# A four-block conditioned sequence model on one core: full values kept in PSUM, normalisation and residual sums on GpSimd, loops written out

## The chip, the cores and the metric

One core of one Trainium2 chip runs the kernel. The metric is the device time of the program in microseconds (us); each figure is the median of several runs. All data is float32.

## What is computed

The input x has 16 batches of 256 rows of 256 values. Four conditioned blocks L0 to L3 act on it one after the other. Each is a sum of a residual and gated sub-layers of the same form:

```python
h = layernorm(x) * (1.0 + scale) + shift      # scale, shift, gate from the batch's condition
x = x + gate * (gelu(h @ W1 + b1) @ W2 + b2)   # the feed-forward form
```

L1 puts an attention of 16 heads of 64 ahead of its feed-forward part, L3 an attention of one head of 256. In L2 the first sub-layer's sum replaces x only where a mask (one bit per batch and row) says so. L3's last sub-layer has a second gelu after W2.

## The kernel before

x stays in SBUF for the whole program (128 partitions, 16 batches of 512 columns). The work is eight stages, p in the code:

- stages 0, 1, 3, 4, 5 and 7 are feed-forward (hidden widths 256, 512, 1024, 512, 512, 1024). A group is two batches; a stage has 8 groups. A chunk is 128 hidden units, so a group has 2, 4 or 8 chunks.
- stage 2 is the attention of 16 heads (one pass over the 16 heads per batch), stage 6 the attention of one head.

Products are made exact enough by splitting: every operand is a high part (rounded to fp32r) and a low part, the full value less the high part. `split3` (L255) issues three matmuls for each product. So each activation is evaluated twice on ScalarE, once as the full value and once rounded, and VectorE subtracts.

**One chunk** passes through `ff_hidden` (L547: six 512-wide matmuls into a U bank of PSUM; two U banks), `ff_activate` (L559: full value into hf, rounded value into hh, both from the U bank), `ff_rest` (L570: hl = hf - hh on VectorE) and `ff_output` (L575: twelve 256-wide matmuls into the Y banks; two pairs of banks, used in turn by the groups). Hidden products run two chunks ahead of output products (LOOK = 2).

**One batch's layer norm** passes through `ln_stats` (L306: statistics on VectorE, then the epsilon addition, L326), `ln_rsqrt` (L328: power -0.5 on GpSimd), `ln_norm` (L332: xn = (x - mean) * rstd on VectorE, two instructions), `ln_transpose` (L365: four transposes by TensorE into a T bank), `ln_modulate` (L379: ScalarE, full value into nf and rounded value) and `ln_rest` (L393: the low part on VectorE). Stage 0 and the start of stage 1 have one T bank, the others two; a transpose waits until ScalarE has read the bank (ln_nf).

**One group's residual**: `ff_take` (L596) multiplies the Y bank by the gate into upd on VectorE; GpSimd has made xb = x + gate * bias (L798) meanwhile; `ff_add` (L607) adds them on VectorE. In stage 4 it copies x into act2, copies the mask column into mcur, adds, lets `copy_predicated` overwrite act2 where the mask is set, and copies act2 back to x. In stage 7 ScalarE applies the second gelu (`ff_gelu2`), GpSimd the gate (`ff_gate2`, L644) and VectorE adds (L614).

**The order of the work** is written out by hand: `ff_body` (L693) lists for each engine what it issues in each chunk c of group g. VectorE begins a group with `ff_take` of the group before, does the statistics in chunk 0 or 1, `ln_norm` and the rounding of the next stage's weights (`weights_hi`, L283) in the chunk after, and `ff_add` in chunks 1 to 3. GpSimd does the powers, the weights' low parts (`weights_lo`, L292) and xb. SP issues the loads of gates and weights and the stores. In stage 2, `mh_vector` (L1192) puts `ln_norm` for the next batch into slot 8 of 16 and `mh_gpsimd` (L1226) the power into slot 5; in stage 6, `sh_turn` (L1386) puts `ln_norm` between the low part of v and the score maximum. The inner groups or batches of stages 1 to 7 are hardware loops (`Fori`) with waits against register values; the first and last ones, and all of stage 0, are straight code. Small `memset` instructions on a spacer tile stand between some of VectorE's dependent instructions. Between stages that aren't both feed-forward all engines meet (`end_phase`).

## Time and profile before

| | |
|---|---|
| median of 3 runs | 1963.29 us (1960.59 to 1963.70) |
| profiled execution, span | 1962.5 us |
| TensorE matmuls busy | 1801.1 us (92%) |
| VectorE busy | 1591.7 us (81%) |
| ScalarE busy | 1304.6 us (66%) |
| GpSimd busy | 869.5 us (44%) |
| DMA queues | 12% of 16 engines' span |
| chain that ended last | PE 57%, DVE 20%, issue 12%, ACT 8% |

The span is the time from the first to the last instruction of one profiled execution; the program's own time isn't listed apart for it, and the median of the runs lies 0.8 us above the span. In the rows PE is TensorE, DVE VectorE, ACT ScalarE, POOL GpSimd; L573 is line 573 of the kernel. Names of tiles stand without their buffer numbers, so "bank" is any of the eight banks of PSUM.

### The profile page before, as it was taken

What the parts mean: (1) busy time and instruction counts of PE and PEld (TensorE: products, weight loads), DVE (VectorE), ACT (ScalarE), POOL (GpSimd) and SP (SyncE); (2) the same over time, 40 slices, a digit from 0 to 9 for tenths busy, and PEclk for the clock granted to TensorE, in tenths of its full rate; (3) what the DMA queues carried; (4) which work ended last, traced back from release to release, by engine and by line L of the source; (5) the groups of instructions that cost most, each with busy time, mean ns of one, the idle gap of its engine ahead of it and who ended that gap; (6) DMA issues with size and microseconds to landing.
All of it is one profiled execution on the core that took longest, in us unless ns stands there. A gap on an engine that the chain in (4) does not pass through costs nothing.

```text
span 1962.5 us, 42453 instructions
## 1 busy us (share of the span) xinstructions
PE 1801.1 (92%) x12739; PEld 1656.6 (84%) x12739; DVE 1591.7 (81%) x4130; ACT 1304.6 (66%) x3178; POOL 869.5 (44%) x1009
## 2 busy tenths in 40 slices
PE   6888979999999999999999989999988989989998
PEld 3657879898999999899999988999877879978997
DVE  5888878999999999999999985555899878995563
ACT  3545557777777787777777775555655646656664
POOL 1445545565555555555555543322333533231111
PEclk7999989999999999999999999999999999999999
DMA  8222200000000000000000001110111111211111
GB/s 278 62 62 79 66 18 8 5 8 8 8 8 5 8 3 8 8 8 8 5 8 3 8 7 31 30 37 25 33 42 36 52 44 33 48 41 44 44 43 43
DMA packets 110877, 64.63 MB, mean 33 GB/s; under 512 B 81530, under 2 KB 92788, under 8 KB 110788
## 3 DMA queue, kind: packets, MB, share of 16 engines
q1 hardware_dynamic: 110788, 63.54, 11.9%
q8 instruction: 45, 0.74, 0.2%
q14 instruction: 44, 0.36, 0.1%
HBM read 59.06 MB, written 4.46 MB: 32 GB/s over the span
## 4 chain that ended last, share of the span: by engine, by line
PE 57%; DVE 20%; issue 12%; ACT 8%; DVEq 1%; POOL 1%; DMA 0%; ACTq 0%; POOLq 0%; SPq 0%
PE bank L257 18%; PE bank L258 17%; PE bank L259 17%; DVE smax L1000 4%; PE bank L1042 3%; ACT prob L1014 2%; DVE xn L338 2%; DVE ptlo L1055 2%; PE bank L375 1%; ACT nf L388 1%; PE bank L434 1%; DVE nTlo L395 1%; DVE hl L573 1%; DVE stats L316 1%; DVE x L637 1%
## 5 line engine op out<-in xcount | busy, mean ns | idle before, releaser
L567 ACT ACTIVATE hf<-bank,vecs 128x512 f32<-128x512 f32 x240 | 167.9, 700 | 311.7 <-PE bank L259 305.7
L573 DVE TENSOR_TENSOR hl<-hf,hh 128x512 fp32r<-128x512 f32 x240 | 199.5, 835 | 157.1 <-ACT hh L567 155.4
L1014 ACT ACTIVATE prob<-bank,nmax 128x256 f32<-128x256 f32 x544 | 253.8, 474 | 92.3 <-DVE nmax L1005 92.2
L330 POOL TENSOR_TENSOR rstd<-vareps,mhalf 128x2 f32<-128x2 f32 x128 | 107.0, 836 | 352.4 <-DVE vareps L326 352.2
L967 POOL TENSOR_TENSOR kklo<-qkf,kkhi 128x256 fp32r<-128x256 f32 x128 | 94.2, 736 | 311.1 <-DVE kkhi L953 311.1
L258 PE MATMUL bank<-WBlo,hh 128*128 128x256 f32 x768 | 218.0, 284 | 0.0
L259 PE MATMUL bank<-WBhi,hh 128*128 128x256 f32 x768 | 217.7, 284 | 0.0
L257 PE MATMUL bank<-WBhi,hl 128*128 128x256 f32 x768 | 217.3, 283 | 0.0
L967 POOL TENSOR_TENSOR qzlo<-qkf,qzhi 64x256 fp32r<-64x256 f32 x256 | 208.3, 814 | 10.0
L257 PE MATMUL bank<-pthi,vlo 128*64 128x256 f32 x512 | 159.7, 312 | 48.1 <-ACT of L1074 30.0
L1031 ACT ACTIVATE prob<-prob,rinv 128x256 f32<-128x256 f32 x272 | 138.7, 510 | 94.7 <-DVE rinv L1024 92.7
L1000 DVE TENSOR_REDUCE smax<-bank 128x2 f32<-128x512 f32 x272 | 186.0, 684 | 11.2 <-PE bank L259 9.6
L1051 ACT ACTIVATE pthi<-bank 128x512 fp32r<-128x512 f32 x272 | 161.1, 592 | 42.3 <-PE bank L1042 42.1
L1055 DVE TENSOR_TENSOR ptlo<-bank,pthi 128x512 fp32r<-128x512 f32 x272 | 185.5, 682 | 1.0 <-ACT pthi L1051 0.8
L257 PE MATMUL bank<-nThi,WBlo 128*128 128x512 f32 x384 | 159.1, 414 | 29.1 <-DVE nTlo L395 17.8
L388 ACT ACTIVATE nf<-bank,mod 128x256 f32<-128x256 f32 x256 | 147.6, 577 | 50.2 <-PE bank L375 35.6
L257 PE MATMUL bank<-aThi,WAlo 128*128 128x256 f32 x576 | 164.9, 286 | 11.6 <-DVEq L247 9.1
L567 ACT ACTIVATE hh<-bank,vecs 128x512 fp32r<-128x512 f32 x240 | 167.2, 697 | 0.0
L1042 PE MATMUL bank<-ident,prob 128*128 128x128 f32 x1088 | 164.7, 274 | 2.3 <-DVE prob L1026 2.3
L259 PE MATMUL bank<-aThi,WAhi 128*128 128x256 f32 x576 | 163.9, 285 | 0.0
L258 PE MATMUL bank<-aTlo,WAhi 128*128 128x256 f32 x576 | 163.8, 284 | 0.0
L258 PE MATMUL bank<-nTlo,WBhi 128*128 128x512 f32 x384 | 154.7, 403 | 0.0
(169 smaller groups left out, 6270.8 us busy)
## 6 DMA issues: line engine op xcount, KB each, us to landing
gates<-gate_scratch SPq DMA_DIRECT2D x96, 256.0 KB, 3.5
agate<-gate_scratch SPq DMA_DIRECT2D x32, 256.0 KB, 3.1
stage<-in_L_cond_W SPq DMA_DIRECT2D x64, 64.0 KB, 2.2
out<-x SPq DMA_DIRECT2D x16, 256.0 KB, 2.2
adaw<-in_L_cond_Wc SPq DMA_DIRECT2D x1, 3072.0 KB, 17.7
stage<-in_L_cond_W_qkv SPq DMA_DIRECT2D x8, 384.0 KB, 3.4
x<-in_x SPq DMA_DIRECT2D x1, 2560.0 KB, 16.9
stage<-in_L_cond_ff_w SPq DMA_DIRECT2D x32, 64.0 KB, 2.1
```

Source lines behind the costliest of these rows:

```text
L257: pe.matmul(dst, lhs[1], rhs[0], start=start, stop=False, skip_group_check=True)
L258: pe.matmul(dst, lhs[0], rhs[1], start=False, stop=False, skip_group_check=True)
L259: return pe.matmul(dst, lhs[0], rhs[0], start=False, stop=stop, skip_group_check=True)
L388: last = act.activation(dst, T[:, c * SEQ:(c + 1) * SEQ], ACT.Identity, scale=mod[:, p, 0, c, bass.ds(b, 1)], bias=mod[:, p, 1, c, bass.ds ...
L567: last = act.activation(dst[:, :], U_BANKS[c % 2][:, :], ACTF[p], bias=vecs[:, at:at + 1])
L573: dve.tensor_tensor(hl[r][:, :], hf[r][:, :], hh[r][:, :].bitcast(F32), ALU.subtract).then_inc(h_lo, 1)
L967: return pool.tensor_tensor(dst, src, hi.bitcast(F32), ALU.subtract)
L1000: dve.tensor_reduce(smax[i][:, :], src.rearrange("p (q k) -> p q k", q=TPB), AX_X, ALU.max).then_inc(max_ready, 1)
L1014: last = act.activation(dst[:, q, :], src[:, q * SEQ:(q + 1) * SEQ], ACT.Exp, scale=scale, bias=nmax[i][:, q:q + 1], accum_out=rsum[i][:, ...
L1042: last = pe.transpose(PTB[i][:, c * SEQ + q * P:c * SEQ + (q + 1) * P], src[:, q, c * P:(c + 1) * P], ident[:, :])
L1051: act.activation(pt[i][0][:, :], PTB[i][:, :], ACT.Copy).then_inc(pt_hi, 1)
L1055: dve.tensor_tensor(pt[i][1][:, :], PTB[i][:, :], pt[i][0][:, :].bitcast(F32), ALU.subtract).then_inc(pt_lo, 1)
```

## The change

- **Full values in place.** nf and hf are gone. ScalarE writes the rounded value first and then the full value back over the bank it reads; VectorE subtracts from there. The T bank and the U bank are now held until VectorE's subtraction is done. There are four U banks (0 to 3) in a ring and one pair of Y banks (4 and 5): the first output of a group waits, bank by bank, for `ff_take` of the group before.
- **Normalisation on GpSimd.** The epsilon addition and `ln_norm` move there. The power and the epsilon addition are done for both batches of a group at once, behind the statistics of both.
- **Residual sums on GpSimd.** `ff_add` runs at the head of GpSimd's list in the next group (in stage 7 behind `ff_gate2`), ahead of the norms, the weights and xb. At the end of a stage that isn't followed by a feed-forward one, and at the end of stage 7, it is the last item.
- **Masked rows.** In stage 4 GpSimd writes the sum into act2 and VectorE's `ff_where` copies the masked rows from there straight into x, in chunks 2 and 3; the copies of x and of the mask are gone.
- **Loops written out.** The `Fori` loops are Python loops, and the spacer memsets are gone.

```diff
-        meanvar = [sb(f"meanvar{j}", [P, TPB, 2]) for j in range(GB)]
-        vareps = [sb(f"vareps{j}", [P, TPB]) for j in range(GB)]
-        rstd = [sb(f"rstd{j}", [P, TPB]) for j in range(GB)]
-        mhalf = sb("mhalf", [P, TPB])
+        meanvar = sb("meanvar", [P, GB, TPB, 2])
+        vareps = sb("vareps", [P, GB, TPB])
+        rstd = sb("rstd", [P, GB, TPB])
+        mhalf = sb("mhalf", [P, GB, TPB])
...
-        nf = [sb(f"nf{j}", [P, ROWW]) for j in range(GB)]
...
-        hf = [sb(f"hf{i}", [P, GW], scope=ffn) for i in range(HRING)]
...
-            if p and early(b, 2 * GB + 2):
+            if p:
...
-            dve.wait_ge(ln_mv, u + 1)
-            dve.tensor_scalar(vareps[j][:, :], meanvar[j][:, :, 1], EPS[p], None, ALU.add).then_inc(ln_ve, 1)
-        def ln_rsqrt(pool, p, b, j):
-            pool.wait_ge(ln_ve, p * BATCH + b + 1)
-            pool.tensor_tensor(rstd[j][:, :], vareps[j][:, :], mhalf[:, :], ALU.pow).then_inc(ln_rstd, 1)
-        def ln_norm(dve, p, b, j):
+        def ln_rsqrt(pool, p, b, j, n=1):
             u = p * BATCH + b
-            dve.wait_ge(ln_rstd, u + 1)
+            pool.wait_ge(ln_mv, u + n)
+            pool.tensor_scalar(vareps[:, j:j + n, :], meanvar[:, j:j + n, :, 1], EPS[p], None, ALU.add).then_inc(ln_ve, n)
+            pool.wait_ge(ln_ve, u + n)
+            pool.tensor_tensor(rstd[:, j:j + n, :], vareps[:, j:j + n, :], mhalf[:, j:j + n, :], ALU.pow).then_inc(ln_rstd, n)
+        def ln_norm(pool, p, b, j):
+            u = p * BATCH + b
+            pool.wait_ge(ln_rstd, u + 1)
             if not early(u, sets(p, b)):
-                dve.wait_ge(ln_tp, u + 1 - sets(p, b))
+                pool.wait_ge(ln_tp, u + 1 - sets(p, b))
             for k in range(TPB):
-                last = dve.tensor_scalar(xn[j][:, k * D:(k + 1) * D], x[:, bass.ds(b * ROWW + k * D, D)],
-                                         meanvar[j][:, k, 0:1], rstd[j][:, k:k + 1], ALU.subtract, ALU.mult)
+                last = pool.tensor_scalar(xn[j][:, k * D:(k + 1) * D], x[:, bass.ds(b * ROWW + k * D, D)],
+                                         meanvar[:, j, k, 0:1], rstd[:, j, k:k + 1], ALU.subtract, ALU.mult)
             last.then_inc(ln_xn, 1)
...
+        def pool_norms(pool, units):
+            if units:
+                ln_rsqrt(pool, *units[0], len(units))
+            for n in units:
+                ln_norm(pool, *n)
...
-                pe.wait_ge(ln_nf, u if p == 0 or p == 1 and early(b, 2 * GB + 1) else u + 1 - sets(p, b))
+                pe.wait_ge(ln_lo, u if p == 0 or p == 1 and early(b, 2 * GB + 1) else u + 1 - sets(p, b))
...
-                for dst in (nf[j][:, c * SEQ:(c + 1) * SEQ], hi[c]):
+                for dst in (hi[c], T[:, c * SEQ:(c + 1) * SEQ]):
...
-            dve.tensor_tensor(lo, nf[j][:, :].rearrange("p (c r) -> p c r", c=DC), hi.bitcast(F32),
+            dve.tensor_tensor(lo, t_bank(p, b, j)[:, :].rearrange("p (c r) -> p c r", c=DC), hi.bitcast(F32),
...
-        U_BANKS, Y_BANKS = bank[0:2], [bank[2:4], bank[4:6]]
+        U_BANKS, Y_BANKS = bank[0:HRING], bank[4:6]
...
-            if not early(n, 2):
-                pe.wait_ge(h_act, n - 1)
+            if not early(n, HRING):
+                pe.wait_ge(h_lo, n + 1 - HRING)
...
-            for dst in (hf[r], hh[r]):
-                last = act.activation(dst[:, :], U_BANKS[c % 2][:, :], ACTF[p], bias=vecs[:, at:at + 1])
+            for dst in (hh[r], U_BANKS[r]):
+                last = act.activation(dst[:, :], U_BANKS[r][:, :], ACTF[p], bias=vecs[:, at:at + 1])
...
-            dve.tensor_tensor(hl[r][:, :], hf[r][:, :], hh[r][:, :].bitcast(F32), ALU.subtract).then_inc(h_lo, 1)
+            dve.tensor_tensor(hl[r][:, :], U_BANKS[r][:, :], hh[r][:, :].bitcast(F32), ALU.subtract).then_inc(h_lo, 1)
...
-            if c == 0 and not early(GROUP_BASE[p] + g, 2):
-                pe.wait_ge(y_taken, GB * (GROUP_BASE[p] + g - 1))
             for r in range(GB * TPB):
-                last = split3(pe, Y_BANKS[i][r // TPB][:, (r % TPB) * D:(r % TPB + 1) * D],
+                if c == 0 and r % TPB == 0 and not early(GROUP_BASE[p] + g, 1):
+                    pe.wait_ge(y_taken, GB * (GROUP_BASE[p] + g - 1) + r // TPB + 1)
+                last = split3(pe, Y_BANKS[r // TPB][:, (r % TPB) * D:(r % TPB + 1) * D],
...
+        def ff_add(pool, p, g):
+            for j in range(GB):
                 n = GB * (GROUP_BASE[p] + g) + j
                 b = GB * g + j
                 if p == L3_FF:
-                    dve.wait_ge(gated2, n - GB * GROUP_BASE[L3_FF] + 1)
-                    dve.tensor_tensor(xs(b), xs(b), act2[:, j, :], ALU.add).then_inc(x_new, 1)
+                    pool.wait_ge(gated2, n - GB * GROUP_BASE[L3_FF] + 1)
+                    pool.tensor_tensor(xs(b), xs(b), act2[:, j, :], ALU.add).then_inc(x_new, 1)
                     continue
-                dve.wait_ge(y_taken, n + 1)
-                dve.wait_ge(xb_ready, n + 1)
+                pool.wait_ge(y_taken, n + 1)
+                pool.wait_ge(xb_ready, n + 1)
                 if p == L2_SSM:
-                    dve.memset(spacer[:, 2 + j:3 + j], 0.0)
-                    dve.tensor_copy(act2[:, j, :], xs(b))
-                    dve.tensor_copy(mcur[:, j, :], maski[:, bass.ds(b * TPB, TPB)])
-                    dve.tensor_tensor(upd[:, j, :], upd[:, j, :], xb[:, j, :], ALU.add).then_inc(x_tmp, 1)
-                    dve.wait_ge(x_tmp, 2 * b + 1)
-                    dve.memset(spacer[:, 4 + j:5 + j], 0.0)
-                    for k in range(TPB):
-                        last = dve.copy_predicated(act2[:, j, k * D:(k + 1) * D],
-                                                   mcur[:, j, k:k + 1].to_broadcast([P, D]),
-                                                   upd[:, j, k * D:(k + 1) * D])
-                    last.then_inc(x_tmp, 1)
-                    dve.wait_ge(x_tmp, 2 * b + 2)
-                    dve.memset(spacer[:, 6 + j:7 + j], 0.0)
-                    dve.tensor_copy(xs(b), act2[:, j, :]).then_inc(x_new, 1)
+                    pool.tensor_tensor(act2[:, j, :], upd[:, j, :], xb[:, j, :], ALU.add).then_inc(x_tmp, 1)
                 else:
-                    dve.tensor_tensor(xs(b), upd[:, j, :], xb[:, j, :], ALU.add).then_inc(x_new, 1)
+                    pool.tensor_tensor(xs(b), upd[:, j, :], xb[:, j, :], ALU.add).then_inc(x_new, 1)
+        def ff_where(dve, p, g, batches=range(GB)):
+            for j in batches:
+                b = GB * g + j
+                dve.wait_ge(x_tmp, b + 1)
+                for k in range(TPB):
+                    last = dve.copy_predicated(x[:, b * ROWW + k * D:b * ROWW + (k + 1) * D],
+                                               maski[:, b * TPB + k:b * TPB + k + 1].to_broadcast([P, D]),
+                                               act2[:, j, k * D:(k + 1) * D])
+                last.then_inc(x_new, 1)
...
-                            for n in norms:
-                                ln_norm(eng, *n)
...
-                        if C == GB and c == 1 and prev:
-                            ff_add(eng, *prev)
-                        if C > GB and 2 <= c < 4 and prev:
-                            ff_add(eng, *prev, [c - 2])
+                        if 2 <= c < 4 and prev and prev[0] == L2_SSM:
+                            ff_where(eng, *prev[:2], [c - 2])
...
-                    for n in norms:
-                        ln_rsqrt(eng, *n)
+                    if prev and p == L3_FF:
+                        ff_gate2(eng, p, g - 1, 1 - i)
+                    if prev:
+                        ff_add(eng, *prev[:2])
+                    pool_norms(eng, norms)
...
-            with eng.Fori(1, GROUPS // 2 - 1) as pair:
-                for i in range(2):
-                    body(eng, p, 2 * pair + i, i, 2)
+            for g in range(2, GROUPS - 2):
+                body(eng, p, g, g % 2, GROUPS - 1 - g)
...
-                if i == 8 and not last:
-                    ln_norm(dve, A, b + 1, 0)
...
+                    ln_norm(pool, A, b + 1, 0)
...
-            with eng.Fori(1, BATCH - 1) as b:
+            for b in range(1, BATCH - 1):
...
-                    ln_norm(eng, *sh_batch(b + 3), n)
...
+                    ln_norm(eng, *sh_batch(b + 3), n)
...
-            with eng.Fori(1, BATCH // 2 - 2) as pair:
-                for i in range(2):
-                    sh_turn(name, eng, 2 * pair + i, i, 3)
+            for b in range(2, BATCH - 4):
+                sh_turn(name, eng, b, b % 2, BATCH - 1 - b)
```

## Rows read from the trace of the kernel before

**Rows 1.** Table of stretches: start:end, length, busy (instructions) per engine, clock, DMA, GB/s.
```profile
20.00:144.70 124.70, 100.85 (x485) 69.60 (x486) 93.31 (x302) 63.85 (x121) 47.23 (x50) 0.86 0.37 110
144.70:253.25 108.55, 93.46 (x589) 84.23 (x587) 93.36 (x188) 59.55 (x110) 62.14 (x45) 0.95 0.26 73
298.27:1093.98 795.71, 753.98 (x5998) 723.55 (x5997) 723.24 (x1822) 623.18 (x1794) 455.69 (x561) 1.00 0.03 7
1211.91:1375.43 163.52, 163.52 (x1063) 149.17 (x1062) 96.65 (x246) 95.39 (x168) 48.05 (x56) 1.00 0.12 32
1375.43:1500.88 125.45, 109.09 (x662) 98.34 (x661) 112.77 (x351) 73.09 (x135) 45.47 (x46) 0.93 0.13 38
1500.88:1602.64 101.76, 93.58 (x600) 84.34 (x599) 89.82 (x241) 61.82 (x115) 51.70 (x56) 0.98 0.18 49
1635.87:1734.93 99.06, 94.02 (x750) 89.52 (x749) 93.55 (x266) 66.14 (x166) 31.83 (x44) 1.00 0.21 44
1765.00:1962.50 197.50, 189.29 (x1208) 171.88 (x1208) 108.05 (x226) 115.58 (x201) 33.14 (x31) 0.98 0.14 43
55.81:144.69 88.88, 73.66 (x382) 52.52 (x382) 73.53 (x228) 43.13 (x82) 39.18 (x40) 0.92 0.24 62
1529.18:1541.54 12.36, 12.36 (x82) 11.17 (x81) 10.86 (x30) 8.60 (x16) 6.57 (x7) 1.00 0.19 52
1210.97:1234.39 23.42, 23.42 (x155) 21.36 (x153) 14.07 (x41) 13.69 (x24) 8.32 (x12) 1.00 0.22 57
```

**Rows 2.** Groups by line: output and inputs, count, busy us, mean ns, idle before.
```profile
L573 DVE TENSOR_TENSOR hl<-hf,hh 128x512 fp32r<-128x512 f32 x240 | 199.5, 835 | 157.1 <-ACT hh L567 155.4 <-issue 0.3
...
L1055 DVE TENSOR_TENSOR ptlo<-bank,pthi 128x512 fp32r<-128x512 f32 x272 | 185.5, 682 | 1.0 <-ACT pthi L1051 0.8
...
L330 POOL TENSOR_TENSOR rstd<-vareps,mhalf 128x2 f32<-128x2 f32 x128 | 107.0, 836 | 352.4 <-DVE vareps L326 352.2
...
L338 DVE TENSOR_SCALAR xn<-x,meanvar,rstd 128x256 f32<-128x256 f32 (+1 forms) x256 | 104.2, 462 | 3.1 <-POOL rstd L330 3.0
...
L967 POOL TENSOR_TENSOR kklo<-qkf,kkhi 128x256 fp32r<-128x256 f32 x128 | 94.2, 736 | 311.1 <-DVE kkhi L953 311.1
...
L977 POOL TENSOR_TENSOR vlo<-vf,vhi 128x512 fp32r<-128x512 f32 x64 | 82.9, 1295 | 25.1 <-DVE vhi L959 24.8 <-POOL qzlo L967 0.4
...
L395 DVE TENSOR_TENSOR nTlo<-nf,nThi 128x512 fp32r<-128x512 f32 x96 | 69.2, 721 | 52.3 <-ACT nThi L388 52.3
...
L604 DVE TENSOR_TENSOR upd<-bank,gates 128x512 f32<-128x512 f32 x96 | 61.6, 683 | 4.2 <-PE bank L259 2.3 <-DVE x L635 0.3
...
L637 DVE TENSOR_TENSOR x<-upd,xb 128x512 f32<-128x512 f32 (+1 forms) x64 | 49.6, 790 | 0.0
...
L1582 POOL TENSOR_SCALAR_AFFINE_SELECT ident<-ident 128x128 f32<-128x128 f32 x1 | 0.3, 293 | 0.2 <-POOL ident L1580 0.2
```

**Rows 3.** Instructions in order of time, VectorE and GpSimd, stage 1 (start, us).
```profile
184.34 2.33 DVE L573 TENSOR_TENSOR hl<-hf,hh 128x512 fp32r<-128x512 f32 x1
...
184.04 3.23 POOL L296 TENSOR_TENSOR WAlo<-stage,WAhi 128x768 f32 x2 [2.37 <-DVE WAhi L289]
```

**Rows 4.** Groups by line: the masked residual of stage 4 on VectorE.
```profile
L629 DVE COPY_PREDICATED act<-mcur,upd 128x256 f32<-128x256 int32 x32 | 13.5, 476 | 0.7
...
L625 DVE TENSOR_TENSOR upd<-upd,xb 128x512 f32<-128x512 f32 x16 | 10.9, 683 | 0.0
...
L635 DVE COPY x<-act 128x512 f32<-128x512 f32 (+1 forms) x16 | 6.8, 423 | 0.7
```

**Rows 5.** In order of time, VectorE and weight loads, one batch of stage 2.
```profile
469.06 0.88 DVE L338 TENSOR_SCALAR xn<-x,meanvar,rstd 128x256 f32 x2
...
472.59 0.13 PEld L257 LDWEIGHTS bank<-pthi,vlo 128*64 128x64 f32 x1 [1.29 <-issue]
```

**Rows 6.** In order of time, VectorE, one batch of stage 6.
```profile
1681.04 0.73 DVE L338 TENSOR_SCALAR xn<-x,meanvar,rstd 128x256 f32 x2
```

**Rows 7.** In order of time, VectorE, the last two additions of stage 7.
```profile
1957.46 2.34 DVE L614 TENSOR_TENSOR x<-x,act 128x512 f32<-128x512 f32 x2 [1.51 <-POOL act L648]
```

More of the change, by code:

```diff
@@ L344, in head_norms @@
             for n in heads(p):
-                if name == "gpsimd":
-                    ln_rsqrt(eng, *n)
-                else:
+                if name == "vector":
                     ln_stats(eng, *n)
-            if name == "vector":
-                for n in heads(p):
-                    ln_norm(eng, *n)
+            if name == "gpsimd":
+                pool_norms(eng, heads(p))
+        def pool_norms(pool, units):
[3 more added lines that the diff above has]
+                ln_norm(pool, *n)
         def t_bank(p, b, j):
@@ L551, in ff_hidden @@
                 pe.wait_ge(ln_lo, p * BATCH + GB * g + GB)
-            if not early(n, 2):
-                pe.wait_ge(h_act, n - 1)
+            if not early(n, HRING):
+                pe.wait_ge(h_lo, n + 1 - HRING)
             for k in range(DC):
-                last = split3(pe, U_BANKS[c % 2][:, :], [w[:, k, c * P:(c + 1) * P] for w in w1],
+                last = split3(pe, U_BANKS[ring(p, i, c)][:, :], [w[:, k, c * P:(c + 1) * P] for w in w1],
                               [m[:, k, :] for m in nT[i]], k == 0, k == DC - 1)
@@ L603, in ff_take @@
                 half = 1 if p == L3_FF else 0
-                dve.tensor_tensor(rows_of(upd[:, j, :]), rows_of(Y_BANKS[i][j][:, :]), gate_row(i, j, half),
+                dve.tensor_tensor(rows_of(upd[:, j, :]), rows_of(Y_BANKS[j][:, :]), gate_row(i, j, half),
                                   ALU.add if half else ALU.mult).then_inc(y_taken, 1)
-        def ff_add(dve, p, g, i, batches=range(GB)):
-            for j in batches:
+        def ff_add(pool, p, g):
+            for j in range(GB):
                 n = GB * (GROUP_BASE[p] + g) + j
@@ L712, in body @@
                     units, norms = [], []
-                if isinstance(g, int) and g == 1 and follows and name == "vector":
-                    eng.wait_ge(x_new, GB * GROUP_BASE[p])
                 slices = [0, 1] if first else [g + 1] if left > 0 else []
@@ L785, in body @@
                 if name == "gpsimd":
-                    for n in norms:
-                        ln_rsqrt(eng, *n)
+                    if prev and p == L3_FF:
[3 more added lines that the diff above has]
+                    pool_norms(eng, norms)
                     for s in slices[:1]:
                         weights_lo(eng, p + 1, s)
-                    if p == L3_FF:
-                        if prev:
-                            ff_gate2(eng, p, g - 1, 1 - i)
-                    else:
+                    if p != L3_FF:
                         for j in range(GB):
@@ L803, in body @@
                         ff_gate2(eng, p, g, i)
+                    if left == 0 and not goes_on:
+                        ff_add(eng, p, g)
                 if name == "sync":
@@ L838, in ff_norms @@
                     ln_stats(eng, *n)
-                for n in ns:
-                    ln_norm(eng, *n)
             if name == "gpsimd":
-                for n in ns:
-                    ln_rsqrt(eng, *n)
+                pool_norms(eng, ns)
         def ff_start(name, eng, p):
@@ L1421, in sh_turn @@
                 if left >= 1:
-                    ln_norm(eng, *sh_batch(b + 3), n)
-                if left >= 1:
                     score_max(eng, b + 1, S1[:, :], 0, SCALE1, H0)
@@ L1443, in sh_start @@
                     ln_rsqrt(eng, S6, b, j)
+                    ln_norm(eng, S6, b, j)
                 if name == "vector" and b == 2:
                     ln_stats(eng, S6, b, j)
-                    ln_norm(eng, S6, b, j)
                 if b == 1:
@@ L1561, in _ @@
             dve.wait_ge(x_loaded, 16)
-            dve.memset(spacer[:, 1:2], 0.0)
             head_norms("vector", dve, 0)
@@ L1578, in _ @@
         def _(pool):
-            pool.memset(mhalf[:, :], -0.5)
+            pool.memset(mhalf[:, :, :], -0.5)
             pool.memset(ident[:, :], 0.0).then_inc(ident_zero, 1)
```

10 lines of the change are left out of this document (1 added, 9 removed).

## The prediction

> **What bounds the kernel now.** I read the table of stretches first. Each stretch runs from one stage's last evacuation of Y to the next one's, so its length is what the stage costs. The last two rows of [rows 1] are the yardstick: in one group of stage 5 and one of stage 3 TensorE is busy for the whole 12.36 us and 23.42 us at granted clock 1.00. A group of four chunks can't take less than 12.36 us, one of eight not less than 23.42. Against that: stage 1 takes 108.55 us for 8 groups (13.57 each), stage 4 125.45 (15.68 each), stage 5 101.76; stage 3 takes 163.52 for seven groups (23.36), all of it TensorE. In the heads of stage 2 TensorE is busy 753.98 of 795.71 us, idle 41.7 us or 3.0 in each of 14 batches; in stage 6 it is idle 5.0 of 99.06 us. Where TensorE idles, VectorE is nearly full: 93.4 of 108.6, 112.8 of 125.5, 723 of 796, 93.6 of 99.1 us. So stages 1, 4 and parts of 0, 2, 5 and 6 are VectorE's; 3 and 7 are TensorE's.
>
> The groups by line say why VectorE is full [rows 2]. The same 128x512 subtraction costs 835 ns on average with both inputs in SBUF (hl) and 682 with one in PSUM (ptlo, upd). A pair of rows shows the difference [rows 3]: one hl takes 2.33 us while GpSimd works for 3.23 us on its weights. The same happens to x (790 ns).
>
> **The parts of the change, summed by stage.** The units:
> - hl 835 to about 682 and nTlo 721 to 682 [rows 2], since one input is now PSUM.
> - Off VectorE: four xn a group (462 ns each), two epsilon additions, two x additions (790).
> - Onto GpSimd: those. An addition 128x512 costs 1295 there (vlo). The two powers (836 each) become one of four columns; I take 0.85. The epsilon addition I take at 0.2.
> - xn on GpSimd is the unknown, no row shows it. Above stands the two-input 128x256 row (kklo, 736 ns), below the one-input 128x128 row (the mask of the identity, 293 ns) doubled less its fixed part, about 0.45. From 736 and 1295 the fixed part of a two-input operation is 0.18 us and 2.2 ns a column; one input is nearer the lower end: 0.55 us.
>
> The Trainium skill (GPSIMD Engine Reference, section 4.1) speaks against the move: it gives elementwise work to VectorE and calls GpSimd about twice as slow with two inputs, about line rate with one. Twice the xn row would be 0.8 us; that price is close to the first rival's.
>
> GpSimd's load in a group then is: old busy time (47.2, 62.1, 45.5, 51.7 us by eight for stages 0, 1, 4, 5), less 0.84, plus 0.2, 2.6 and 2.2, plus 0.7 for waits on its own results: 10.8, 12.6, 10.5, 11.3 us. Only stage 1, with its 1024 columns of weights a group, lies over 12.36.
>
> **Stage 1**: 12.5 instead of 13.57 a group: -9 us. Bounds: -11.6 (TensorE's floor, 97 with a shorter last group) and 0.
>
> **Stage 4**: VectorE loses two copies of x, the sum (683), the copy back (423) and the mask copy, and keeps four predicated copies (476) [rows 4]. With xn, the epsilon additions and the shorter hl it falls from 14.1 to about 7.6 us a group. The chain sum, norms, weights, then xb waiting for x, then the next sum, runs through GpSimd in about 12.4 us. I take 12.5: -25 us; bounds -26.6 and -15.
>
> **Stage 5**: the first group (17.8 us, still behind stage 4's last masks) comes to the floor, the others lie on it: -4, bounds -5 and 0.
>
> **Stage 0**: groups last 12.7 us (seven in the stretch of 88.88 us), with the conditioning steps between them, on VectorE and TensorE in turn, partly at half clock. VectorE gives up some 3.5 us a group, but the only transpose bank is now held until VectorE's subtraction (0.68) rather than ScalarE's last write, and GpSimd needs 10.8. I take -6; bounds -14 and +6.
>
> **Stage 2**: per batch the two xn (0.88) lie right ahead of a score maximum; the subtraction after them is what TensorE waits for, 1.29 us, once a batch [rows 5]. That, the epsilon addition and the shorter aTlo are worth 1.4 us. Against it, GpSimd's xn now runs in slot 5 beside VectorE's casts of q and k, which want the same ports: up to two operations of 0.55 delay them by about half a microsecond. Net -0.9 in 15 batches: -13. Bounds -30 (two thirds of TensorE's idle 3.0) and 0.
>
> **Stage 6**: xn (0.73 for two) goes from between vlo and the maximum [rows 6], TensorE has 0.46 us of slack a batch: 0.4 by 16, -6; bounds -8 and 0.
>
> **Stages 3 and 7**: nothing inside. **Edges**: x is summed by GpSimd at 1.3 instead of 0.69, which shows where nothing covers it: +1 at the ends of stages 1 and 5; at the end of stage 7 both gates come first and both sums behind them, so the last x ends about 1.6 us later than now [rows 7]; +1 where stage 3 starts and +0.5 for stage 7, since both statistics are awaited before one power. Together +5; bounds +3 and +9.
>
> **Costed at nothing.** Four U banks: a looser wait than before. One pair of Y banks: the next group's first output must wait for upd (0.68), and TensorE has eight transposes and six 512-wide matmuls (2.3 us) in between; if upd starts as late as 1.8 us after them, as in some groups of stage 5, the stall is 0.2 us, 7 us over 48 groups. ScalarE's second result written to PSUM: no row has ScalarE writing there; it is busy 8.6 of 12.36 us [rows 1]. SP: no transfer is added or removed, and they wait on the same x.
>
> Loops written out: no wait on a register's value, no jump. The two kinds stand side by side in the trace, in rows already read: stage 3's 163.52 us hold straight groups and looped ones, all TensorE. So 0, bounds -5 and +5. The Trainium skill (Runtime: NRT & Kernel Launch, Instruction fetch mechanics) says that a taken branch out of the fetched window costs a stall, which would make writing out a gain; the trace doesn't show one at the looped groups, and I add nothing.
>
> Sum: -6 - 9 - 13 - 25 - 4 - 6 + 5 = -58. The profiled execution has a span of 1962.5 us; the median of the runs, 1963.3, is 0.8 above it. 1962.5 - 58 + 0.8 = 1905.
>
> **Rivals.**
> 1. GpSimd at the upper price: xn costs 0.74 or more, as the two-input row. Then stage 1 needs 13.4 a group (-1 instead of -9), stage 0 gives -3, stage 2 only -5 through contention, edges +6: 1962.5 - 39 + 0.8 = 1924. For it: this engine's power takes 0.84 us for two columns, so nothing on it is cheap. Against: the slope of its rows is all operand reading. The Trainium skill's factor of two would be this case.
> 2. VectorE relieved further than I count: with hl at 682, fewer blocked operations, stage 2 gives -28 and stage 0 -14: 1882. For: most idle time of TensorE in stage 2 ends on VectorE. Against: the new contention in the same slots.
> 3. Slower, by GpSimd as the bound of the small stages. Its place is four xn a group, its price 1.5 us each if an operation with two operands per partition costs like the power. Load then is 7.8 + 0.7 + 6.0 = 14.5, 16.4, 14.3 and 15.1 in stages 0, 1, 4, 5, together 60.3 a round of four groups against 54.7 now (12.7, 13.57, 15.68, 12.7): 8 x 5.6 = +45, less 14 elsewhere: 1994. It decides from 1.26 us on, where 16 more xn make up 54.7 + 1.8 - 36.3. Against: 5 ns a column is twice the two-input slope.
> 4. The stalls only change hands (y, transposes in stage 0, x late for xb), and less than 4 us is left: needs the bounds of all stages at once.
>
> **How the numbers follow.** Forecast 0.50, rival 1 0.24, rival 2 0.15, rival 3 0.08, rival 4 0.03. About 0.2% (4 us) is what a measurement can tell from no change. Faster 0.89, same 0.03, slower 0.08. The range reaches to rival 2 and somewhat past rival 1: 1878 to 1940, which leaves out rival 3 and the tails.
>
> **What would show it.** Right: hl near 682 with no long ones; stage 4 at 12.4 to 12.6 a group; stage 1 with GpSimd nearly without idle time; TensorE's 1.29 us wait in each batch of stage 2 gone; stages 3 and 7 unchanged to 2 us. Wrong: xn on GpSimd above 0.8 us; casts in stage 2 held up more often than before; TensorE waiting for upd at groups' starts, or for nTlo before transposes in stage 0; GpSimd's queue holding up the low parts of q and k.

## The result and the profile after

The changed kernel takes 1971.7 us (median of 4 runs, 1970.9 to 1973.0) where the kernel before takes 1963.5 on the same chip (4 runs, 1960.6 to 1965.9): a ratio of 1.0045, 95% interval 1.0031 to 1.0059. That is 8 us slower. The forecast was 1905 with a range up to 1940, so both the sign and the range were wrong. The profiled execution has a span of 1969.1 us against 1962.5.

First the table of stretches of the changed kernel: start:end, length, then busy time (and instructions) of TensorE, weight loads, VectorE, ScalarE and GpSimd, granted clock, DMA share, GB/s. Each row ends with the evacuation of a stage's last Y; the row of 951.24 us is stage 2 with the first group of stage 3, the one of 186.73 us stage 6 with the first group of stage 7.

```profile
66.49:150.49 84.00, 70.87 (x371) 47.49 (x370) 57.07 (x146) 42.47 (x81) 80.40 (x80) 0.96 0.26 72
150.49:265.37 114.88, 98.25 (x609) 87.68 (x607) 55.22 (x120) 59.82 (x110) 98.54 (x86) 0.96 0.23 65
265.37:1216.61 951.24, 894.16 (x7031) 864.68 (x7032) 799.86 (x2047) 743.75 (x2086) 581.13 (x714) 0.99 0.04 9
1216.61:1380.33 163.72, 163.72 (x1064) 149.31 (x1063) 72.17 (x165) 94.02 (x168) 85.75 (x96) 1.00 0.13 32
1380.33:1497.85 117.52, 102.27 (x636) 90.15 (x635) 69.65 (x173) 70.84 (x131) 94.30 (x95) 0.97 0.16 42
1497.85:1614.48 116.63, 101.50 (x620) 90.16 (x618) 56.92 (x145) 62.90 (x116) 91.77 (x100) 0.94 0.15 42
1614.48:1801.21 186.73, 167.93 (x1269) 159.92 (x1270) 132.59 (x336) 119.00 (x277) 109.38 (x127) 0.96 0.19 41
```

Beside [rows 1]: stage 1 has 114.9 us instead of 108.6, stage 5 116.6 instead of 101.8, stage 4 117.5 instead of 125.5, stage 3 the same. VectorE has been emptied: in stage 1 it is busy 55.2 us instead of 93.4. GpSimd has taken its place: 98.5 of 114.9 us.

Next the groups by line (count, busy us, mean ns, idle before and its releaser):

```profile
L573 DVE TENSOR_TENSOR hl<-bank,hh 128x512 fp32r<-128x512 f32 x240 | 164.6, 686 | 325.6 <-ACT bank L567 325.6
L334 POOL TENSOR_SCALAR xn<-x,meanvar,rstd 128x256 f32<-128x256 f32 x256 | 322.9, 1272 | 9.4 <-PE bank L375 1.1
L621 POOL TENSOR_TENSOR x<-upd,xb 128x512 f32<-128x512 f32 x64 | 81.1, 1288 | 49.0 <-DVE upd L604 49.0
L326 POOL TENSOR_TENSOR rstd<-vareps,mhalf 128x4 f32<-128x4 f32 (+1 forms) x80 | 74.9, 937 | 10.2 <-POOL vareps L324 0.7
```

The costliest new row is xn: 1.27 us an instruction and 323 us in all, where VectorE took 462 ns [rows 2]. hl is at 686 ns and the long ones are gone, as intended. The waits of TensorE and its weight loads (us in total, times, longest), from the view of waits:

```profile
PEld bank L375 <- POOL xn L334: 63.0, 37, 6.1
PE bank L375 <- POOL xn L334: 53.2, 27, 5.9
PE bank L254 <- POOLq L957: 20.1, 15, 1.5
PE bank L254 <- DVE upd L604: 11.9, 6, 4.3
```

The first two describe largely the same stalls, since the transposes of xn load their weights and then stream. L957 is an empty instruction on GpSimd that reports q's low parts as done; in stage 2 it comes after xn and the scores wait for it, once a batch. The fourth is the single pair of Y banks. One group of stage 5 on GpSimd, in order of time (start, duration), shows the new cycle:

```profile
1577.52 2.55 POOL L621 TENSOR_TENSOR x<-upd,xb 128x512 f32<-128x512 f32 x2
...
1582.15 0.23 POOL L324 TENSOR_SCALAR vareps<-meanvar 128x4 f32<-128x4 f32 x1 [2.08 <-DVE meanvar L317]
1582.53 1.04 POOL L326 TENSOR_TENSOR rstd<-vareps,mhalf 128x4 f32<-128x4 f32 x1
1583.67 4.84 POOL L334 TENSOR_SCALAR xn<-x,meanvar,rstd 128x256 f32<-128x256 f32 x4
1588.48 0.88 POOL L292 TENSOR_TENSOR WAlo<-stage,WAhi 128x64 fp32r<-128x64 f32 x3
1589.32 2.55 POOL L785 TENSOR_TENSOR xb<-x,gates 128x512 f32<-128x512 f32 x2
```

The sums are done at 1580.07 (1577.52 + 2.55); then GpSimd waits 2.08 us for VectorE's statistics; then power and four xn take 6 us, and TensorE's second set of transposes waits 1.75 us for them at 1588.57. GpSimd's queue is in order, so even its idle 2 us can't be used for the weights and xb behind xn. From the epsilon addition before (1567.84) to this one are 14.3 us, against TensorE's 12.36.

### The profile page after: what moved, and what is told of

Its sections match the earlier page's. It is cut to its first block, busy times and chain, and to the rows that moved or that the text cites. A ratio compares the mean times of both kernels' runs of the same rounds, so it can differ in the third digit from the quotient of the medians.

```text
span 1969.1 us, 38164 instructions
## 1 busy us (share of the span) xinstructions
PE 1793.7 (91%) x12739; PEld 1652.2 (84%) x12739; DVE 1329.5 (68%) x3313; ACT 1311.0 (67%) x3178; POOL 1244.8 (63%) x1393
## 3 DMA queue, kind: packets, MB, share of 16 engines
q1 hardware_dynamic: 110788, 63.54, 11.9%
## 4 chain that ended last, share of the span: by engine, by line
PE 55%; POOL 16%; DVE 11%; issue 9%; ACT 7%; DMA 1%; POOLq 1%; DVEq 0%; SPq 0%; ACTq 0%
PE bank L254 17%; PE bank L255 16%; PE bank L256 16%; POOL xn L334 8%; PE bank L1026 3%; DVE smax L984 3%; POOL rstd L326 2%; DVE stats L311 2%; ACT bank L388 2%; PE bank L375 2%; ACT prob L998 2%; DVE ptlo L1039 1%; ACT nThi L388 1%; POOL qzlo L951 1%; POOL vlo L961 1%
## 5 line engine op out<-in xcount | busy, mean ns | idle before, releaser
L573 DVE TENSOR_TENSOR hl<-bank,hh 128x512 fp32r<-128x512 f32 x240 | 164.6, 686 | 325.6 <-ACT bank L567 325.6
L334 POOL TENSOR_SCALAR xn<-x,meanvar,rstd 128x256 f32<-128x256 f32 x256 | 322.9, 1272 | 9.4 <-PE bank L375 1.1
L951 POOL TENSOR_TENSOR qzlo<-qkf,qzhi 64x256 fp32r<-64x256 f32 x256 | 198.1, 774 | 10.1
L254 PE MATMUL bank<-kkhi,qzlo 128*128 128x256 f32 x512 | 148.7, 291 | 24.5 <-POOLq L957 20.1
L254 PEld LDWEIGHTS bank<-WBhi,hl 128*128 128x128 f32 x768 | 149.6, 195 | 18.2 <-issue 10.2
L567 ACT ACTIVATE bank<-bank,vecs 128x512 f32<-128x512 f32 x240 | 159.0, 662 | 0.0
```

The lines of the kernel that those rows point to most:

```text
L254: pe.matmul(dst, lhs[1], rhs[0], start=start, stop=False, skip_group_check=True)
L334: last = pool.tensor_scalar(xn[j][:, k * D:(k + 1) * D], x[:, bass.ds(b * ROWW + k * D, D)], meanvar[:, j, k, 0:1], rstd[:, j, k:k + 1], A ...
L567: last = act.activation(dst[:, :], U_BANKS[r][:, :], ACTF[p], bias=vecs[:, at:at + 1])
L573: dve.tensor_tensor(hl[r][:, :], U_BANKS[r][:, :], hh[r][:, :].bitcast(F32), ALU.subtract).then_inc(h_lo, 1)
L951: return pool.tensor_tensor(dst, src, hi.bitcast(F32), ALU.subtract)
```

## The experiments

Every ratio is against runs of the kernel before on the same chip. Three chips were used, and the kernel before has medians of 1961.5, 1963.9 and 1962.5 us on them, so differences of 2 to 3 us between experiments from different chips say nothing. Stage times quoted below are from the same table of stretches, each kernel cut at its own last evacuations. "Changed" is the kernel of the diff; later kernels build on the best so far. Each diff shows the lines that carry the edit.

### Normalisation back on VectorE

```diff
             for n in units:
-                ln_norm(pool, *n)
+                if n[0] not in NORM_DVE:
+                    ln_norm(pool, *n)
...
+                            dve_norms(eng, norms)
```

dve_norms calls ln_norm for the stages in NORM_DVE, at the places of the kernel before; nothing else differs.

> The changed kernel with only xn back on VectorE, in its old places; epsilon, power and sums stay on GpSimd. Theory G (the price of xn on GpSimd, 1.21 us each, makes it the bound of stages 0, 1, 4 and 5): four xn a group are 4.9 us of GpSimd's 12 to 14.5, so groups in stages 1, 4 and 5 fall to 12.4 to 12.8 us, stage 0 by some 8 us; time 1905 to 1920. Rival H (the banks held longer, the single pair of Y banks or the sums on GpSimd are what costs): TensorE goes on waiting at groups' starts and the time stays above 1950.

1921.6 us, ratio 0.979 (0.978 to 0.981): 50 us faster than the changed kernel and 40 faster than the kernel before on the same chip, 1.6 us above theory G's range. Stage 1 falls to 105.8 (13.2 a group, more than G allowed), stage 4 to 101.9, stage 5 to 101.3 us. In stage 0 the last evacuation comes 3.8 us earlier, where G said 8.

```profile
L337 DVE TENSOR_SCALAR xn<-x,meanvar,rstd 128x256 f32<-128x256 f32 x256 | 110.3, 488 | 31.6 <-POOL rstd L327 31.5
```

One part of the change costs more than the whole change loses. The exception is stage 6, 196.3 instead of 186.7 us: there the two xn lie next to GpSimd's products and take up to 1.69 us for two on VectorE, between vlo and the maximum, where [rows 6] had 0.73.

> As the one before, but xn of the two attention stages (2 and 6) stays on GpSimd. Theory G: the same stages 0, 1, 4, 5 as there; stage 2 keeps its 55.8 us a batch and its wait of 1.7 us for the low part of q behind xn. If that wait is xn's doing, the other kernel (xn on VectorE in slot 8) is 5 to 15 us faster than this one; if VectorE is the bound of stage 2 all the same, this one is faster by as much.

Where the engine that makes xn changes between two stages, GpSimd first waits for the xn of the stage before; nothing else is added. With NORM_DVE = [0, 1, 3, 4, 5, 7], 1918.4 us, ratio 0.978 (0.976 to 0.979). The stretch of stage 2 is 944.0 with xn on GpSimd, 936.7 with it on VectorE: 7 us lost, as the wait for the low part of q foretold. Stage 6 is 187.6 against 196.3: 9 won, which the expectation had left out, so in total this kernel is the faster one by 3 us.

### What the instruction costs on GpSimd

```diff
-                                         meanvar[:, j, k, 0:1], rstd[:, j, k:k + 1], ALU.subtract, ALU.mult)
+                                         0.0, 1.0, ALU.subtract, ALU.mult)
```

This kernel leaves the normalisation out (it copies x through two operations), so only its time counts.

> The changed kernel with the mean and the reciprocal deviation replaced by the constants 0 and 1 in xn (so it leaves the normalisation out). It prices the operand form. If the two per-partition operands are what costs, xn falls from 1.21 us to 0.5 to 0.75 us and the time to 1915 to 1935. If it is GpSimd's price for any one-input operation of 256 columns, xn stays near 1.2 and the time within 5 us of the changed kernel.

xn takes 1.07 us (median of the tile's view; mean 1.10), the kernel 1939.7, ratio 0.989 (0.987 to 0.991), so neither branch of the expectation holds. The two pointers together cost 0.15 of the 1.22 us; the rest is the instruction's own.

```diff
-                                         meanvar[:, j, k, 0:1], rstd[:, j, k:k + 1], ALU.subtract, ALU.mult)
+                                         rstd[:, j, k:k + 1], None, ALU.mult)
```

Here the subtraction of the mean is left out.

> The changed kernel with the normalisation on GpSimd as one multiplication by rstd, the subtraction of the mean left out. Theory (each of the two operations of the instruction has its own pass on GpSimd, so half of them is half of the time): xn at 0.6 to 0.7 us instead of 1.27, total 1915 to 1930 us. Rival (the time is that of reading and writing 256 columns, not of the arithmetic): xn at 1.0 to 1.2 us, total 1938 to 1968 us.

xn takes 0.92 us (mean 0.97), the kernel 1926.6, ratio 0.981 (0.979 to 0.982). The groups by line of the two kernels, immediates first:

```profile
L334 POOL TENSOR_SCALAR xn<-x 128x256 f32<-128x256 f32 x256 | 275.5, 1099 | 9.2 <-PE bank L375 2.2
```

```profile
L334 POOL TENSOR_SCALAR xn<-x,rstd 128x256 f32<-128x256 f32 x256 | 245.0, 971 | 11.8 <-PE bank L375 4.0
```

Medians: 1.22 us with two operations and two pointers, 1.07 with two and none, 0.92 with one and one. Neither theory of the last run holds for the price, though the total lies in the first one's range: the second operation with its pointer is worth 0.30 us, and 0.92 remains with one of each. Even that is above the two-input subtraction of 256 columns on the same engine, 0.74. The total follows the price: in the three kernels 1971.7, 1939.7 and 1926.6, that is 32 us for the first 0.15 and 13 for the second.

### The kernel before with the same move

```diff
-            with eng.Fori(1, GROUPS // 2 - 1) as pair:
-                for i in range(2):
-                    body(eng, p, 2 * pair + i, i, 2)
+            for g in range(2, GROUPS - 2):
+                body(eng, p, g, g % 2, GROUPS - 1 - g)
...
             if name == "gpsimd":
...
+                for n in ns:
+                    ln_norm(eng, *n)
```

Loops written out, and xn alone on GpSimd.

> The kernel before with its loops written out and only xn moved to GpSimd (epsilon, sums and banks as before). Theory G: xn costs 1.2 us and more, VectorE gets 1.6 us a group back, GpSimd's load is 10.9 in stage 1 and under 11 elsewhere, so no stage is bound by it alone; 1940 to 1965. Rival H says nothing of banks is in it, so it should gain what VectorE gives up, 1930 or less.

2012.4 us, ratio 1.026 (1.024 to 1.028), slower than either theory allowed. xn costs 1.43 us on average here. From the waits (us in total, times, longest):

```profile
PEld bank L377 <- POOL xn L338: 94.3, 45, 6.0
PE bank L377 <- POOL xn L338: 80.5, 43, 5.8
POOL act L650 <- ACT act L644: 49.8, 3, 19.8
DVE x L616 <- POOL act L650: 31.6, 6, 6.0
```

The last row is what was not foreseen: the sums still sit on VectorE, whose queue stops at them until GpSimd has done the second gate's product, now late behind xn. Stage 7, untouched in every kernel so far (160 us), takes 178.9. Beside the kernel with nothing but its loops written out (the next experiment, 1934.5 us), stages 1, 4, 5 and 7 are 15.5, 10.9, 28.4 and 19.1 us longer. So xn on GpSimd costs 78 us here although banks, sums and full values are as before: the move does its harm without the rest of the change.

### The written-out loops alone

> The kernel before with its hardware loops written out and nothing else changed. Theory (loop ends cost little, and what they cost lies beside other work): 1958 to 1964 us, no measurable change. Rival (each loop end drains the engines for some us): 1945 to 1957 us. Other rival (the longer straight code must be fetched and stalls): 1965 to 1975 us.

1934.5 us, ratio 0.985 (0.983 to 0.987): the loops cost 29 us, in a kernel otherwise the same, and none of the three ranges reached so far. 22.5 us of the profiled execution's 28.6 are the stretch of stage 2 (936.2 instead of 958.7), where a looped batch lasts 56.8 us and a written-out one 55.3. So the next kernel has only that loop written out:

```diff
-            with eng.Fori(1, BATCH - 1) as b:
+            for b in range(1, BATCH - 1):
```

> The kernel before with only the loop over the batches of stage 2 written out. Theory (in a looped batch each wait against a register's value costs VectorE 0.16 us that a wait on a constant does not, eight times ahead of the casts of q alone, 1.5 us in each of 14 batches): the batch 55.3 instead of 56.8 us, stage 2 shorter by 20 to 24 us, the other stages unchanged within 2 us: 1938 to 1944 us. Rival (the gain came from the other stages' loops or from code that lies otherwise in memory): stage 2 within 5 us of before, 1955 to 1964 us.

1938.5 us, ratio 0.988 (0.986 to 0.990); the stretch of stage 2 is 936.4, stages 1, 4 and 5 together 5.4 us shorter (0.8, 1.8 and 2.8), somewhat more than the theory gave them. Stages 0 and 1 run before the edited loop and are 1.5 and 0.8 us shorter all the same, so differences of this size in one stage of one execution are not the edit's. VectorE in order of time shows the difference. Before, in the loop:

```profile
548.35 0.17 DVE L1005 TENSOR_SCALAR nmax<-smax 128x2 f32<-128x2 f32 x1
548.55 0.28 DVE L951 CAST qzhi<-qkf 64x256 fp32r<-64x256 f32 x1
```

With all loops written out:

```profile
538.11 0.17 DVE L1004 TENSOR_SCALAR nmax<-smax 128x2 f32<-128x2 f32 x1
538.19 0.28 DVE L950 CAST qzhi<-qkf 64x256 fp32r<-64x256 f32 x1
```

From nmax to the first cast of q, which waits on values worked out from the loop's register, VectorE takes 0.239 us start to start (mean of 80 in ten batches; most are near 0.205), with constants 0.078. The kernel before has both kinds in one trace, since its first and last batches are straight code. There the distance is 0.078 to 0.080 us, as in the first batch:

```profile
279.22 0.17 DVE L1005 TENSOR_SCALAR nmax<-smax 128x2 f32<-128x2 f32 x1
279.30 0.28 DVE L951 CAST qzhi<-qkf 64x256 fp32r<-64x256 f32 x1
```

Eight such places a batch make 1.29 us, where the batch got 1.54 us shorter. But the lengths of other instructions move too, as they fall differently beside GpSimd's: vhi has a mean of 661 ns in the loop and 415 written out (four a batch, 0.98 us), vareps 648 and 170 (0.48 us). Together that is more than the batch gained, so part of it only turned into waits elsewhere. TensorE's waits for ptlo in the stretch of stage 2 fall from 16.9 us (16 of them) to one of 1.6 us; over ten batches TensorE is idle 20.6 instead of 29.9 us and busy 532.2 instead of 538.3. How much of the gain is the 0.16 us and how much that new alignment was not separated.

### Sums, and what is left

```diff
                         if c == stats_at + 1:
...
+                        if C == GB and c == 1 and prev:
+                            ff_add(eng, *prev[:2])
+                        if C > GB and 2 <= c < 4 and prev:
+                            ff_add(eng, *prev[:2], [c - 2])
```

> The changed kernel with both the normalisation and the residual sums of the feed-forward stages on VectorE in every stage: what is left of the change is full values in place in PSUM, the banks, the masked rows straight into x, and the written-out loops. Theory (sums on GpSimd are covered and only unload VectorE, by 1.9 us for each of the feed-forward groups beside TensorE's 12 us a group): stages 0, 1, 4 and 5 stay within 1 us of the run with xn alone on VectorE, 1918 to 1928 us. Rival (sums on GpSimd hold the VectorE's statistics and the next group back): faster than that run, 1905 to 1917 us. Other rival (VectorE is close to the bound and has no room): stages 1, 4, 5 longer by 1 us a group, 1935 to 1950 us.

1944.6 us, ratio 0.991 (0.989 to 0.993): the "other rival" for stages 1 and 4. They take 113.1 and 118.2 us; stage 5 stays at 101.8. So the sums on GpSimd are worth 23 us. And this kernel is 10 us slower than the kernel before with its loops written out, from which it differs by values in place, banks, masks, epsilon and the merged power on GpSimd, and the missing spacers. Stage 4, with the masks, is 6.4 us shorter than there (118.2 and 124.6); stages 0, 1 and 5 are 5.4, 6.7 and 3.3 us longer. Its waits say where:

```profile
PE bank L255 <- DVE upd L615: 39.7, 21, 5.2
```

With one pair of Y banks TensorE can't start a group's output until VectorE has taken the last one, and a VectorE that also does sums and norms is late for it, 21 times. That the single pair is what costs is argued from this row; the next experiments test it.

### The best placement, and the PSUM parts taken singly

> The changed kernel with xn on VectorE in every stage but 6, where GpSimd keeps it. Theory (stages are independent, each stage takes what the engine that makes xn costs there): stages 0 to 5 as with xn on VectorE everywhere, stage 6 as in the changed kernel (187 instead of 196 us of the stage table), so 1912 us (1908 to 1917). Rival (stage 6 was slow there for another reason, or stage 7 gives it back): 1919 to 1923 us, as with xn on VectorE everywhere.

With NORM_DVE = [0, 1, 2, 3, 4, 5, 7], 1911.0 us, ratio 0.974 (0.972 to 0.975); stage 6 is 185.3, the others as on VectorE everywhere. The three kernels that follow start from it.

```diff
-        U_BANKS, Y_BANKS = bank[0:HRING], bank[4:6]
+        U_BANKS, Y_BANKS = bank[0:2], [bank[2:4], bank[4:6]]
...
-            if not early(n, HRING):
-                pe.wait_ge(h_lo, n + 1 - HRING)
+            if not early(n, 2):
+                pe.wait_ge(h_lo, n - 1)
```

> The best kernel so far (xn on VectorE in every stage but 6: 1911 us) with the banks of before: 2 for U, 2 pairs for Y; the full values stay in place in their U bank, which is therefore held until VectorE's subtraction. Theory (the single pair's waits for upd, 14.3 us in 6 places, are real, but with two U banks held for longer TensorE waits for hl instead): 1911 to 1935 us. Rival (two U banks are enough and the waits for upd come back): 1898 to 1908 us.

1904.1 us, ratio 0.970 (0.969 to 0.972), the fastest of all, and the rival's case: the waits for upd are gone. From its table of stretches (stages 1, 4, 5, and the last seven groups of stage 7):

```profile
147.69:246.94 99.25, 92.25 (x593) 83.91 (x592) 62.83 (x142) 59.24 (x110) 67.61 (x61) 0.96 0.26 75
...
1348.60:1447.30 98.70, 98.54 (x648) 89.92 (x647) 78.13 (x205) 70.43 (x132) 58.47 (x64) 1.00 0.18 50
1447.30:1545.37 98.07, 93.34 (x607) 85.19 (x605) 64.04 (x169) 61.91 (x116) 62.81 (x77) 0.98 0.18 50
...
1731.99:1897.59 165.60, 160.02 (x1033) 145.01 (x1031) 68.48 (x140) 95.10 (x169) 41.59 (x38) 1.00 0.14 42
```

All three four-chunk stages now last about 8 groups of TensorE's 12.36 us (98.9). Stages 1, 4 and 5 are together 12.9 us shorter than with one pair; stage 7, with eight chunks, is 5.4 us longer, and stage 0 ends 3.4 us later. In stage 7 TensorE's hidden products now wait for U banks that are held until VectorE is done, a wait that the kernel of 1911 us, with four, doesn't have there:

```profile
PE bank L255 <- DVE hl L584: 4.3, 5, 1.1
```


```diff
-            for dst in (hh[r], U_BANKS[r]):
+            for dst in (hf[r], hh[r]):
...
-            dve.tensor_tensor(hl[r][:, :], U_BANKS[r][:, :], hh[r][:, :].bitcast(F32), ALU.subtract).then_inc(h_lo, 1)
+            dve.tensor_tensor(hl[r][:, :], hf[r][:, :], hh[r][:, :].bitcast(F32), ALU.subtract).then_inc(h_lo, 1)
```

> The best kernel so far (1911 us) with the full hidden values written to SBUF, as before, and not in place in PSUM; the banks stay as changed. Theory (in place helps by keeping hl out of GpSimd's way): hl 0.83 to 0.88 us on average instead of 0.685, VectorE busy longer by 35 to 45 us, of which stages 0, 1, 4 and 5 show some: 1915 to 1930 us. Rival (hl lies beside TensorE's work and its length is covered now that VectorE has lost the sums): 1909 to 1914 us.

1926.4 us, ratio 0.982 (0.980 to 0.983): hl is back at 865 ns and 15 us are lost, as the theory had it. TensorE's waits for upd grow from 14.3 us (6 of them) to 23.5 (19). GpSimd pays as well: its sums take 1384 ns on average instead of 1293.

> The best kernel so far (1911 us) with both: full hidden values in SBUF and the banks of before (2 for U, free again after ScalarE; 2 pairs for Y). What is left of the change in the feed-forward network is then the sums on GpSimd, the masked rows straight into x and the written-out loops. Theory (each of the two parts in PSUM pays only through the other): within 5 us of the run with values in SBUF alone, less the 14 us of waits for upd: 1903 to 1920 us. Rival (the long hl now keeps hidden chunks back): 1920 to 1935 us.

1909.0 us, ratio 0.973 (0.971 to 0.975), in the theory's range, with hl at 853 ns. With two pairs for Y, values in place save 5 us; with one pair, 15. The length of hl shows mostly where VectorE is late for the one pair.

```profile
L585 DVE TENSOR_TENSOR hl<-hf,hh 128x512 fp32r<-128x512 f32 x240 | 204.2, 853 | 184.1 <-ACT hh L579 183.6
```

## Why the prediction was wrong

The change is four changes with different signs. By medians, along one chain of kernels (on different chips, hence good to 2 or 3 us):

| from | to | us |
|---|---|---|
| before (1963.5) | loops written out (1934.5) | -29 |
| that | values in place, banks, masked rows into x, epsilon and merged power on GpSimd; norms and sums on VectorE (1944.6) | +10 |
| that | sums on GpSimd (1921.6) | -23 |
| that | norms on GpSimd: the changed kernel (1971.7) | +50 |

The four make +8. The order matters for how much each gets: a part that pays in one kernel pays less in another, as the last two experiments show.

**xn on GpSimd: the step that failed.** I took 0.55 us, between 0.45 and 0.736 and nearer the lower bound. It costs 1.22 us (median, 1.27 on average). The lower bound came from another kind of instruction, a mask of the identity; the upper from the two-input subtraction, on the belief that one input can't cost more than two. The runs say otherwise: 0.92 us with one operation, 1.07 with two and no pointers, 1.22 as written. The range of that term should have gone well past 0.74, since no row showed the form. The Trainium skill (GPSIMD Engine Reference, section 4.1) gives GpSimd about twice VectorE's time for two inputs and about line rate for one; here the one-input instruction takes 2.8 times the 462 ns that VectorE took, so its rule for one input doesn't cover this form. Its direction, elementwise work belongs on VectorE, holds here for xn outside stage 6 and not for the sums: an addition takes 1.29 us on GpSimd, and having them there is worth 23 us.

**Rival 3 is the mechanism that came true**, at a smaller size. It put the turning point at 1.26 us and gave slower from there on; 1.27 was measured and +8 us came out. Its load with 1.27 is 56.7 us a round of four groups instead of 54.7, that is +16, less the 14 elsewhere: +2. That this lies near the measured +8 is partly luck: the sum has nothing for the loops, which gave 29 us back, so the rest of the change cost 37 us. It had the place right (four xn a group in the small stages) and was given a chance of 0.08, since 5 ns a column seemed excluded. The trace has 1.22 us for 256 columns, 4.8 ns a column. The stages differ from its sum: stage 0 takes 12.0 a group where it says 13.6, stage 1 14.4 where it says 15.5, stage 4 14.7 for 13.4 and stage 5 14.6 for 14.2. In the last two the group lasts longer than GpSimd's load, and GpSimd is busy only 94.3 of 117.5 and 91.8 of 116.6 us: it isn't merely full but ordered. In the rows of stage 5 it waits 2 us for statistics between the sums and the power with xb and weights behind.

**Loops: the second failed step.** I wrote 0, with bounds of 5 each way, because stage 3's looped groups ran as fast as its straight ones. That was the wrong place to look: in stage 3 TensorE is the bound and covers whatever VectorE loses. The loop that mattered was the one of stage 2, where the prediction's own table shows VectorE at 723 of 796 us. It cost 24 us by itself. The trace held the sign of it, 0.2 us ahead of each first cast of q in the looped batches and 0.08 in the straight ones, and I didn't read it. The Trainium skill (Runtime: NRT & Kernel Launch, Instruction fetch mechanics) had the direction right and gives another cause, a stall at a taken branch. Here the added distances lie inside the batch, and VectorE doesn't stop at the loop's end: its last nmax of one pass runs from 609.14 to 609.68 us, and the first cast of v of the next starts at 609.59.

**Stage 4** was put at 100.5 us. With xn on VectorE it takes 101.9, with two Y pairs 98.7: the working of what VectorE sheds was right, and xn on GpSimd took 16 of its 25 us back (117.5). **Stage 1** was put at 99.5 us and **stage 5** at 97.8: 99.3 and 98.1 in the best kernel, but 114.9 and 116.6 in the changed one. **Stage 2** was put at -13, for the shorter work of VectorE. The stretch got 7 us shorter; the loop alone gives 22, and written out the stage has the same 936 us in the kernel before and with full values in place and xn on VectorE. A batch takes 56.8 us before, 55.8 in the changed kernel and 55.2 to 55.3 written out with xn on VectorE. The wait of 1.29 us did go, as forecast, but one of 1.4 us for L957 took its place in each batch. So that term was nothing, and the contention and order feared beside it were real: xn on GpSimd costs 7 us there. **Stage 6** was put at -6 and got about that (186.7 instead of 192.2 with a first group of stage 7), and it is the one stage where xn belongs on GpSimd. **Stage 0** was put at -6: its last evacuation comes 4.5 us later. Its seven further groups did get shorter, 84.0 us for 88.9, but the first evacuation came at 66.5 us instead of 57.1, which the sum had not looked at; with xn on VectorE it comes at 61.0. With VectorE relieved and xn on it the last evacuation is at 144.3 us (before: 146.0). **Edges**, put at +5 in all, came to more, as xn stands ahead of the first transposes there: from the last residual of stage 2 to the first evacuation of stage 3 are 37.3 us instead of 31.1, from that of stage 6 to that of stage 7 35.7 instead of 32.3, where the sum had +1 and +0.5. Stage 7 and what follows are 1.4 us longer (160.2 and 7.7 instead of 159.9 and 6.6).

**Single Y pair, costed at nothing** with up to 7 us as a stall: 11.9 us of waits in the changed kernel, 39.7 where VectorE is busier. The sum looked only at how long upd takes. What counts is when VectorE's queue gets to it. Giving the pair back, for two of the four U banks, brought 7 us.

**VectorE's side** was right: hl 686 instead of 835 without long ones, and its busy time fell from 1581 to 1323 us in the stretches (in stage 4 to 8.7 us a group, where the forecast had 7.6). Rival 2, which hoped for more from that, fell with it: VectorE was relieved further than needed and the time went to GpSimd.

**Slips in the sums.** Rival 1's terms add up to -38, not -39, and twice the xn row (462 ns) is 0.92 us, not 0.8. Neither changes the forecast.

Open are: how the 24 us of the loop divide between the longer waits and the new alignment of VectorE and GpSimd; how the 0.30 us between xn's first and last form divide between its pointer and its operation, and why the one-operation form still costs more than a two-input subtraction; and a kernel with two Y pairs in the small stages and four U banks in stage 7, which by its stages should reach about 1899 us (an estimate: 1904.1 less 5.4), was not tried.

## What to carry to other kernels

Before work is moved to an engine, its price there must come from a row of the same form of instruction; if there is none, the range of the term must reach the point where the sign turns, and that point (here 1.26 us) says what to measure first. An engine that relieves the bound must be checked as a queue, in order, with what waits behind each instruction, not as a sum of loads. And a loop should be judged at the stage where its engine is the bound: the same kind of loop cost nothing in stage 3, where TensorE is busy throughout, and 24 us in stage 2, where VectorE is nearly full.

## What the hardware showed beyond that

- On GpSimd a tensor_scalar of 128x256 with two operations takes 1.22 us with two pointers and 1.07 with immediates, with one operation and pointer 0.92, while the two-input subtraction of the same size takes 0.74.
- The power of 128x4 takes 1.04 us on average in the changed kernel. One of 128x2 takes 0.84 before [rows 2] and 0.78 in the changed kernel, so merging two into one saves 0.5 to 0.6 us a group.
- ScalarE's second result written over its own input bank takes 662 ns, the first, into SBUF, 696:

```profile
L567 ACT ACTIVATE hh<-bank,vecs 128x512 fp32r<-128x512 f32 x240 | 167.0, 696 | 326.0 <-PE bank L256 325.8
...
L567 ACT ACTIVATE bank<-bank,vecs 128x512 f32<-128x512 f32 x240 | 159.0, 662 | 0.0
```

- The contention of VectorE and GpSimd falls on both: with hl reading SBUF, hl goes from 685 to 865 ns and GpSimd's sums from 1293 to 1384 on average. The medians stay (693 and 1295): a few long ones make the difference, up to 2.3 and 1.8 us.
